# Starting the next batch's token mix in the closing stage, with a reordered prologue and norm

## What is computed

```python
# token mix, for the 256 image tokens (x: 64 channels x 256 tokens x 4 heads)
q, k, v = proj(Wq), proj(Wk), proj(Wv)
ew, ek = exp(w_bias * local_mask), exp(k)
y = sigmoid(q) * (ew @ (ek * v)) / (ew @ ek)
h = layernorm(y @ out_w + out_b + flatten(x)) * ln_g + ln_b
h = concat([h, W_E[x_txt] * sqrt(256)])            # 128 text rows, gathered
# attention, 16 heads of 16, relative positions in a window of +-4
h = h + attn(layernorm(h)) @ Wo + bo
# 8 experts of width 256, every token through all of them, router weights per token
x2 = layernorm(h)
w = routing_weights(sigmoid(x2 @ Wr / temperature))  # zone weights, else the top two
h = h + sum_e w[:, e] * ((silu(x2 @ Wg[e]) * (x2 @ Wu[e])) @ Wd[e])
```

## Time and profile before

| | |
|---|---|
| median of 3 runs | 1245.3 us (1244.47 to 1248.25) |
| profiled execution | 1249.12 us, span 1247.3 us |
| mean granted TensorE clock | 0.952 of full |
| PE busy | 1020.4 us, 82% of the span |
| DVE busy | 753.0 us, 60% |
| ACT busy | 451.2 us, 36% |
| POOL busy | 247.8 us, 20% |
| chain that ended last | PE 46%, issue 22%, DVE 17%, DMA 5%, ACT 4%, POOL 4% |

### The profile page before, as it was taken

The page is one execution under the profiler, slowest core; times in us unless marked ns, Lnnn a source line. Parts: engine busy times, 40 slices in busy tenths (PEclk is TensorE's granted clock), DMA queues, the critical chain, the costliest instruction groups (busy, mean ns, idle before and its releaser), DMA issues.

```text
span 1247.3 us, 16776 instructions
## 1 busy us (share of the span) xinstructions
PE 1020.4 (82%) x5668; PEld 744.4 (60%) x5668; DVE 753.0 (60%) x1597; ACT 451.2 (36%) x651; POOL 247.8 (20%) x262
## 2 busy tenths in 40 slices
PE   3536698888898798888898798988988888987798
PEld 2412277636786287745786377854876367862687
DVE  7347355774648755685658745685567746487343
ACT  1133512453124723355124622346224531347211
POOL 6228411021200402013200412004120212004000
PEclk9569789989999999999999999999999999999899
DMA  4286203602062110802044020722026020620100
GB/s 110 101 240 174 68 5 97 140 11 53 4 178 59 24 42 33 202 10 39 18 121 115 9 56 0 202 44 39 18 79 157 10 52 5 179 60 18 35 1 13
DMA packets 96962, 87.87 MB, mean 70 GB/s; under 512 B 67281, under 2 KB 85074, under 8 KB 95090
## 3 DMA queue, kind: packets, MB, share of 16 engines
q1 hardware_dynamic: 96524, 86.24, 28.3%
q0 software_dynamic: 384, 1.05, 0.3%
HBM read 60.35 MB, written 26.92 MB: 70 GB/s over the span
## 4 chain that ended last, share of the span: by engine, by line
PE 46%; issue 22%; DVE 17%; DMA 5%; ACT 4%; POOL 4%; SPq 2%; POOLq 0%; DVEq 0%; ACTq 0%
PE S L913 16%; PE S L934 8%; DVE maxima L1220 4%; PE S L844 4%; PE S L779 4%; PE S L827 4%; PE S L741 3%; DVE S L1241 3%; ACT scratch L1033 3%; PE S L658 1%; DMA txt_row<-in_L_txt_W_E,txt_idx 1%; DVE res L1374 1%; PE S L760 1%; SPq L566 1%; PE S L787 1%
## 5 line engine op out<-in xcount | busy, mean ns | idle before, releaser
L1491 POOL TENSOR_TENSOR bands<-scratch,one 64x432 f32<-64x432 f32 x128 | 119.1, 931 | 525.0 <-ACT scratch L1033 519.4
L1070 ACT ACTIVATE silu<-S 128x384 f32<-128x384 f32 x128 | 63.0, 492 | 352.2 <-PE S L913 243.6
L1220 DVE TENSOR_REDUCE maxima<-S 128x2 f32<-128x768 f32 x192 | 172.2, 951 | 19.0 <-PE S L787 17.6
L934 PE MATMUL S<-w_d,hT 128*128 128x256 f32 x768 | 182.0, 382 | 1.5 <-DVE hT L1362 0.7
L1241 DVE TENSOR_TENSOR S<-S,bands 64x144 f32<-64x144 f32 x384 | 154.3, 402 | 43.3 <-PE S L827 32.6
L1033 ACT ACTIVATE scratch<-S 128x768 f32<-128x768 f32 x192 | 154.8, 812 | 56.3 <-DVE S L1241 43.0
L779 PE MATMUL S<-k_st,q_st 128*128 128x384 bf16 x384 | 101.9, 334 | 68.0 <-DVE maxima L1220 39.7
L934 PEld LDWEIGHTS S<-w_d,hT 128*128 128x128 f32 x768 | 143.4, 191 | 22.2 <-issue 2.3
L1362 DVE TENSOR_TENSOR hT<-silu,S 128x384 f32<-128x384 f32 x128 | 70.7, 552 | 116.7 <-PE S L913 97.4
L827 PE MATMUL S<-q_st,k_st 128*128 128x384 bf16 x384 | 98.8, 356 | 40.2 <-ACT scratch L1033 36.7
L1011 ACT ACTIVATE scratch<-scratch 128x816 bf16<-128x816 bf16 x56 | 92.3, 1694 | 41.5 <-DMA scratch<-d_band_t 41.5
(11 more groups left out here) (167 smaller groups left out, 1515.6 us busy)
## 6 DMA issues: line engine op xcount, KB each, us to landing
bands<-d_band_s SPq DMA_DIRECT2D x16, 864.0 KB, 9.4
scratch<-d_band_t SPq DMA_DIRECT2D x8, 1632.0 KB, 9.6
d_parts<-scratch SPq DMA_DIRECT2D x48, 192.0 KB, 1.9
q_st<-d_parts SPq DMA_DIRECT2D x48, 192.0 KB
k_st<-d_parts SPq DMA_DIRECT2D x48, 192.0 KB
d_band_w<-bands SPq DMA_DIRECT2D x32, 240.0 KB, 3.9
out<-scratch SPq DMA_DIRECT2D x8, 384.0 KB, 2.6
x_in<-in_x SPq DMA_DIRECT2D x8, 256.0 KB, 3.6
```

The lines of the kernel that those rows point to most:

```text
L934: mm = pe.matmul(D[:, i // 2, (i % 2) * E:(i % 2 + 1) * E], hT[:, (FT * e + m) % 3, i * P:(i + 1) * P], w_d[:, e, m, :], start=(m == 0), s ...
L1220: dve.tensor_reduce(dst, S[:, c0:c0 + 2, PAD:PAD + T], AX, ALU.max).then_inc(max_done.sem, 1)
L1491: nc.gpsimd.tensor_tensor(bands[rows, :, :, 2 * pair:2 * pair + 2].rearrange("p i w h -> p h i w"), win, one[rows].unsqueeze(2).unsqueeze( ...
```

## The change

`mix_in` leaves the head of the round. A new step `mix_next` in the closing stage does the `mix_in` of batch b + 1, behind the last units and ahead of `rel_values`; in the last round it is left out. For that, `rel_values` writes PSUM banks 6 and 7, and `rel_w`, `rel_p` and `rwt` move in the scratch. `mix_sums` now stands ahead of `turn_x2`. The first image tile's ln_g and ln_b stay on GpSimd, the second's go to VectorE. The router's ranking is cut in two and moves behind `turn_norm`, and the preparation of constants in round 0 too. The hidden tiles get a fourth slot, with units in a new order. SP issues the band ahead of the k loads. The prologue loads x first, and the bias rows and the reordering later; the memsets of q and k are written as float32 and come after GpSimd's gather.

```diff
+HSLOTS = 4
...
-FILL_MIX = [("residual", 0), ("mix_in", 0), ("turn_x2", 0), ("mix_sums", 0), ("router", 1),
-            ("mix_out", 0), ("router_zone", 1), ("mix_norm", 1), ("router_rank", 2),
-            ("norm_stats", 2), ("router_pick", 1), ("turn_norm", 2), ("project_qk", 0),
-            ("project_rel", 1), ("project_v", 15)]
-FILL_MAXIMA = [0, 0, 1] * 8
+FILL_MIX = [("residual", 0), ("mix_sums", 0), ("turn_x2", 0), ("router", 1),
+            ("mix_out", 0), ("router_zone", 1), ("mix_norm", 1), ("norm_stats", 3), ("turn_norm", 1),
+            ("router_rank", 1), ("router_order", 0), ("router_pick", 2), ("project_qk", 0),
+            ("project_rel", 2), ("project_v", 13)]
+FILL_MAXIMA = [0, 1, 1] + [0, 0, 1] * 7
...
-FILL_OUT = [("turn_outputs", 3), ("turn_attn", 6), ("turn_weights", 1), ("rel_values", 1)]
+FILL_OUT = [("turn_outputs", 3), ("turn_attn", 6), ("turn_weights", 2), ("mix_next", 0), ("rel_values", 0)]
...
-        units = [("gate", 0), ("up", 0), ("gate", 1), ("up", 1)]
+        units = []
+        for n in range(HSLOTS):
+            units += [("gate", n), ("up", n)]
         for e in range(NE):
-            if e + 1 < NE:
-                units += [("gate", 2 * e + 2), ("up", 2 * e + 2)]
-            units += [("down", e, 0), ("down", e, 1)]
-            if e + 1 < NE:
-                units += [("gate", 2 * e + 3), ("up", 2 * e + 3)]
+            parts_e = [("down", e, 0), ("down", e, 1)]
+            n = FT * e + HSLOTS
+            if n < FT * NE:
+                parts_e += [("gate", n), ("up", n), ("gate", n + 1), ("up", n + 1)]
+            units += parts_e
...
+            if not ffn:
+                steps.append(("mix_in",))
             for name, n in FILL_MIX:
+                if name == "mix_norm":
+                    flush()
...
-                if name == "mix_out" and not ffn:
+                if name == "turn_norm" and not ffn:
                     steps.append(("prepare",))
...
             for name, n in FILL_OUT:
+                if name == "mix_next":
+                    fill(len(left))
+                    flush()
+                    if not more:
+                        continue
...
 (SP, prologue)
                 if not later(b):
                     load_x(b)
+                    load(0)
+                    bias_rows()
                     load(1)
-                    sp.wait_ge(rows_ordered, 3 * 16)
+                    order_rows()
                     load(2)
...
 (SP, project_rel)
                 stack(q_st, 0, Q_PART)
-                sp.wait_ge(k_out.sem, k_out.at(b, 3))
-                stack(k_st, 3, K_PART)
                 sp.wait_ge(proj_pe.sem, proj_pe.at(b, 10))
                 sp.wait_ge(rel_t_out.sem, rel_t_out.at(b, P // BT))
                 sp.dma_start(band_t.rearrange("p i w h -> p i (w h)"),
...
+                sp.wait_ge(k_out.sem, k_out.at(b, 3))
+                stack(k_st, 3, K_PART)
...
 (TensorE)
+            def mix_next(b):
+                pe.wait_ge(at_act.sem, at_act.at(b, KT))
+                pe.wait_ge(rw_act.sem, rw_act.at(b, KT))
+                mix_in(b + 1)
...
             def rel_values(b):
-                pe.wait_ge(at_act.sem, at_act.at(b, KT))
+                if later(b):
+                    pe.wait_ge(silu_done.sem, silu_done.at(b - 1, NE * FT))
+                    pe.wait_ge(h_done.sem, h_done.at(b - 1, NE * FT))
...
-                    pe.matmul(S[:, g, 0:T], rel_v[:].rearrange("p h d -> p (h d)"), rwt[:, g],
+                    pe.matmul(S[:, 6 + g, 0:T], rel_v[:].rearrange("p h d -> p (h d)"), rwt[:, g],
...
 (ScalarE)
+            def mix_next(b):
+                act.wait_ge(win_done.sem, win_done.at(b, WINS * AH // 2))
+                act.wait_ge(pv_done.sem, pv_done.at(b, AH // GRP))
+                mix_in(b + 1)
...
 (VectorE, mix_norm)
                 norm(b, mix_dve, mix_root, mixed, lambda i: hid[:, i], IT)
+                dve.wait_ge(mix_dve.sem, mix_dve.at(b, 5 + 3 * IT))
+                dve.tensor_tensor(hid[:, 1], hid[:, 1], ln_g[:], ALU.mult).then_inc(hid_second.sem, 1)
+                dve.wait_ge(hid_second.sem, hid_second.at(b, 1))
+                dve.tensor_tensor(hid[:, 1], hid[:, 1], ln_b[:], ALU.add).then_inc(hid_second.sem, 1)
...
 (VectorE, maxima, n == 0)
-                    dve.tensor_copy(band_h[:, :, 0:2], band_t[:, :, :, 0:2].rearrange("p i w h -> p i h w")
-                                    ).then_inc(band_first.sem, 1)
+                    dve.wait_ge(k_out.sem, k_out.at(b, 3))
+                    for h in range(2):
+                        dve.tensor_copy(band_h[:, :, h], band_t[:, :, :, h]).then_inc(band_first.sem, 1)
...
 (GpSimd)
+            def mix_next(b):
+                pool.wait_ge(win_done.sem, win_done.at(b, WINS * AH // 2))
+                mix_in(b + 1)
```

More of the change, by code:

```diff
@@ L73 @@
 WINS = P // BL
-N_LOADS = (9, 4, 10 + 3 + NJ)
+N_LOADS = (6, 4, 10 + 3 + NJ)
 N_ZERO = 6
@@ L972, in turn_norm @@
             def turn_norm(b):
-                if not later(b):
-                    act.wait_ge(consts, N_CONSTS)
                 for k in range(KT):
@@ L981, in project_qk @@
             def project_qk(b):
+                if not later(b):
+                    act.wait_ge(consts, N_CONSTS)
                 for n in range(4):
```

104 lines of the change are left out of this document (61 added, 43 removed).

## The result

| | before | after |
|---|---|---|
| median | 1246.8 us (4 runs, 1244.5 to 1260.4) | 1312.9 us (4 runs, 1306.1 to 1323.0) |
| ratio | | 1.0513, 95% interval 1.0411 to 1.0615 |
| span of the profiled execution | 1247.3 us | 1311.7 us |
| mean granted TensorE clock | 0.952 | 0.914 |
| a round, the last five full ones | 143.3 to 143.4 us | 153.6 to 156.7 us |

The change made the kernel 5.1% slower. The forecast was 1290.0, range 1252 to 1305: the direction was right, the size 23 us short, and the result lies outside the range. (The median before, 1246.8 us, is that of the four runs made beside the result; the 1245.3 above comes from three.)

What follows compares the result with a forecast made beforehand. TensorE was taken as full in the closing stage, with some 7 us a round open to a better order. Terms summed to +44.7 on the profiled 1249.1 us, giving 1293.8, or 1290 for the median; range 1252 to 1305.

Steps and rivals of the forecast that it cites:

- +5.6: Closing stage: the moved mix_in starts the residual 5.6 us later, for six rounds 33.6; between 5.3 and 6.0.
- The first-named rival: The clock holds: without the 28.0 us of clock cost the time is 1262 (1250 to 1272); chance 0.18.
- the one that the norm window closes: Rival: the window between mix_out and projection falls under 11.8 us, 1234 with the clock held; chance 0.08.
- The remaining units of the experts are the same eleven: Closing stage: expert units left there stay the same eleven, so only mix_in's 5.69 us are added.
- +3.6: Closing stage of round 0, without expert units: mix_in costs 5.6 and 0.6, a warm residual gives back 2.6.
- +3.3: turn_x2 to gate unit at half clock after a 4.8 us gap: +3.3 a round, 23.1 in seven; bounds 1.8 and 3.8.
- slower still: Rival: slow stretches join through mix_out (up to 0.8 a round), k loads land later (1.2); about 1304, chance 0.06.
- -1.2: Projection to first maxima: band issued ahead of six k loads wins 1.2 us a round, 8.4 in seven; bounds 0 and -2.9.
- The norm window: mix_out's end to projection: 14.7 us for 16.56, -1.8 a round (-2.5 to -0.5); +0.7 for slow clock.
- -2.5 a round: Norm window by the skill's rule, VectorE about twice GpSimd's speed: -2.5 a round, total 4.6 us lower.
- The prologue: Once only: x loaded first gives 3.9 us, norm no longer behind constants 1.6, split tiles 0.9; -6.4 (-3 to -8).
- the prediction's estimate by width: Norm window: by width, a 256-wide VectorE operation beside GpSimd takes about 1.05 us, its pair ending at about M+5.5.

Runs made afterwards that it cites:

- moved: bestC with the token mix moved into the closing stage and VectorE's turn_x2 part ahead of its mix_sums part; 1269.31 us, ratio 1.0177.
- bestC: bestA with the hidden product owed when the projections start put ahead of them on VectorE, no moved mix; 1229.34 us, ratio 0.9849.
- mix_back: Changed kernel with mix_in put back between residual and turn_x2, and mix_sums behind turn_x2, on every engine; 1243.28 us, ratio 0.9967.
- bestA: mix_back with the unit order, hidden slots, fillers and banks of before the change; 1237.03 us, ratio 0.9923.
- dup_order: dve_order with fewer maxima fillers, mix matmuls repeated unused behind the residual, and TensorE's turn_x2 ahead of mix_sums; 1278.76 us, ratio 1.0231.
- dve_order: Changed kernel with VectorE's part of turn_x2 ahead of its part of mix_sums from round 1 on; 1289.59 us, ratio 1.0334.
- moved_order: moved with TensorE's turn_x2 ahead of mix_sums; 1270.97 us, ratio 1.0164.

## Why the prediction was wrong in size

The forecast was 22.9 us short. The terms below make 19.8 of that; the other 3.2 is the step from the profiled execution to the median, taken as 3.8 from the kernel before and 0.6 in the changed one.

**What held.** The reading on which it rested: TensorE is full in the closing stage, and the moved mix had stood where TensorE would wait. moved against bestC gives +5.5 a round for the closing stage (forecast +5.6) and next to nothing won behind the residual. The chain behind it came as written: the wait ahead of turn_x2 was 4.42 (4.8 forecast), turn_x2 began at R+10.7 (10.8), the clock was already at half there. The first-named rival, that the clock holds, is out, and so is the one that the norm window closes.

**"The remaining units of the experts are the same eleven": wrong.** This is the step that failed first, and the largest part of the miss: the closing stage's "+5.6" measured +7.0. The last units are eleven again, but the new order has a down part among them where a gate unit was (TensorE is busy 23.40 us instead of 22.5 in moved), and the waits on silu (0.33) and VectorE (0.40) are longer than those of the old order. That is 24.93 against 23.46 in moved, 1.5 a round, and 1.5 again in mix_back against bestA. The closing stages came out 10.1 above forecast: 8.3 in the six rounds with units, and 1.8 in the first, which has none and cost +5.4 for a forecast of +3.6.

**"+3.3" for the clock: too small, its bound too.** The term ended with the gate unit, its upper bound (3.8) with mix_out's first part. In four rounds the half clock lasted through all of mix_out and nearly two units more (633.2 to 649.2 at 0.50 in the round shown), and mix_out took 6.9 us instead of 5.3. The stretch averaged 25.9 instead of 24.7. In all that is 5.4 above forecast and not 8, because the first round took 23.7 already before the change, where the sum had 21.15 for all seven. I took the tail as the pattern, and read from it only where the clock fell, not how long it stayed down: there it is low for some 10 us, beyond the gate unit, as in three rounds of the change. The four rounds with 20.5 us stand in no row of before. Two slow stretches that join through mix_out were part of the "slower still" rival; 0.06 was too little for it, and even its 1304 is short of the result.

**"-1.2" to the maxima: wrong for a reason I had named.** "The transfers as a whole are the same and should end at about 660.0" made the k loads as early as the band had been. They ended late, TensorE waited 2.33, and only 0.4 a round was won (5.6 above forecast). What I had not seen is that the clock falls inside the maxima in every other round, within 1.5 us of the end of this wait: 34.4 for 32.8. The wait alone does not decide it: 2.33, 2.37 and 3.04 us were followed by a fall, 2.32 and 2.36 were not. From there, and from the unit order again, come the 5.0 above forecast in maxima and attend.

**The norm window** was forecast at 14.7 with 0.7 for its clock. It was 14.7 in four rounds and 15.8 in three, in all 3.4 better than forecast; 1.5 of that is one slow round of before (18.0), which the forecast had left out. Counted from mix_out's end (646.03), VectorE's pair ended at +5.35 (5.5 forecast) and turn_norm began at +9.24 (655.27 in the trace; 9.3 forecast). These two numbers are right by luck, as the last rows of this section show: VectorE's pair is not slowed in proportion to its width, it stands behind GpSimd's. The 4.6 by which the prediction has the total lower at -2.5 a round is 4.9 by its own terms (0.7 times seven).

**The prologue** gained 9.3, not 6.4, and the first turn_norm began at 39.28 (44.8 forecast): the term had the input's load and missed that VectorE was held up by GpSimd. Before the change, on VectorE and then on GpSimd:

```profile
7.24 5.08 DVE L1090 CAST scratch<-scratch 128x512 f32<-128x512 uint8 x1
...
12.36 0.69 DVE L1093 TENSOR_TENSOR scratch<-scratch 128x512 f32<-128x512 f32 x1
12.97 4.71 DVE L1097 COPY resid<-ident 64x64 f32<-64x64 f32 x4
```

```profile
6.84 5.21 POOL L1397 MEMSET q_st<- 128x6144 bf16 x1
12.11 5.37 POOL L1399 MEMSET k_st<- 2x6144 bf16 x1
```

After, on VectorE, with the clears later on GpSimd:

```profile
7.25 0.42 DVE L1128 CAST scratch<-scratch 128x512 f32<-128x512 uint8 x1
...
8.32 0.48 DVE L1135 COPY resid<-ident 64x64 f32<-64x64 f32 x4
```

The cast took 5.08 us and ended 0.27 behind GpSimd's clear, the four copies 4.71 and ended 0.20 behind the next one; with no clear beside them they take 0.42 and 0.48. The two-input operation between them was not held: it took 0.69 beside the clear and without it. What I had read as slow operations were waits. The Trainium skill (SBUF — State Buffer, SBUF: two separate sides) says that VectorE and GpSimd share a pair of ports of which one instruction holds the whole for its full length, while the other waits; on VectorE's side this concerns its two-port modes, and operations with two SBUF inputs where GpSimd's reads SBUF too. These rows agree (a clear reads nothing), and so does the norm window of the changed kernel, here on GpSimd:

```profile
649.47 0.74 POOL L1496 TENSOR_TENSOR hid<-hid,ln_g 128x256 f32<-128x256 f32 x1 [1.10 <-DVE hid L1153]
650.29 0.81 POOL L1498 TENSOR_TENSOR hid<-hid,ln_b 128x256 f32<-128x256 f32 x1
...
655.29 1.84 POOL L1508 TENSOR_TENSOR hid<-hid,bo_all 128x768 f32<-128x768 f32 x1 [1.17 <-DVE scratch L1153]
```

VectorE's operation at 655.60 took 1.75 us, where one of this width takes 0.36 alone: it ended at 657.35, 0.22 behind GpSimd's. The pair at 649.87 and 650.53 ended at 650.49 and 651.38, each 0.28 behind GpSimd's (650.21 and 651.10). The contended 0.79 of the earlier trace rows is the same: it ended at 620.85, 0.22 behind GpSimd's 620.63. So an operation of VectorE that is held ends shortly behind GpSimd's (0.22 us at a width of 192, 0.28 at 256), and the prediction's estimate by width is the wrong rule.

## What to carry to other kernels

Before work is moved to an earlier stage, look at what it covers where it stands: matmuls that run while TensorE would otherwise wait for another engine cost nothing, and in a full stage they cost their whole length (+5.5 here), while the wait that they had covered comes back (the stretch stayed at 20.8 to 22.8 us for 21.1). Idle TensorE time then costs a second time through the clock. The full clock came back only when all of the gaps were filled with matmuls (dup_order), and spare ones won no time over a better order on VectorE (dve_order) in that stretch beyond 3 us in seven rounds. Where units are reordered, count again which of them fall into each full stage.

## What was not expected of the hardware

- The half clock can outlast the idle time ahead of it by far: 16.00 us at 0.50 with TensorE busy 16.00 (633.20 to 649.20 in the change). In moved_order, with a wait of 4.77, the mean of 0.85 over 22.73 us makes only some 6.8 us at half clock (0.30 of the stretch). The Trainium skill (TensorE: Matmul & The Clock Gate, HAM oscillation — how this bites in real kernels) tells how waits bring the clock down at each tile. The waits of 4.42 and 4.77 agree with that; in dve_order the clock fell behind shorter ones, 1.32 and 1.49 us with short matmuls between.
- Small changes elsewhere shift in which rounds the clock falls. The norm window of before has it full in six of seven rounds, that of bestC in two, although bestC waits less there (one wait of 2.0 us and one of 0.5 or none, for three of 1.5, 1.5 and 2.1). What sets that is not settled.
- GpSimd's clear of two partitions of 6144 bf16 took as long (5.37) as that of all 128 (5.21); the clear of all 128, written as 3072 float32 a partition, took 2.65 in the changed kernel.
